# Layer 0 of a spectral convolution: two PSUM banks for the Hilbert rows, base bank first, and the low half by TensorE and ScalarE

## The reference

```python
# layer 0, on g = _gn(x)
X = jnp.fft.rfftn(g, axes=(-2, -1), norm='backward')
Yr = _rconv(Xr, wr) - _rconv(Xi, wi) + b_real[:, None, None]
Yi = _rconv(Xr, wi) + _rconv(Xi, wr) + b_imag[:, None, None]
x = x + jnp.fft.irfftn(lax.complex(Yr, Yi), axes=(-2, -1), norm='backward')
# layer 1, on g = _gn(x)
x = x + mean filter of 15 x 15 (g)
```

## Time and profile before

| | |
|---|---|
| median of 3 runs | 3912.32 us (3907.86 to 3915.44) |
| the profiled execution's own time | 3906.01 us |
| its span | 3904.2 us |
| busy: TensorE, VectorE | 3305.6 us (85%), 3271.4 us (84%) |
| busy: GpSimd, ScalarE | 2633.2 us (67%), 1926.4 us (49%) |

### The profile page before, as it was taken

One profiled execution on the slowest core, in us unless ns is written; L12 is line 12 of the kernel. 1 busy time (PEld: TensorE's weight loads), 2 busy tenths in 40 slices (PEclk: granted clock), 3 DMA queues, 4 the chain that ended last, 5 costly groups with the idle time before them and its releaser, 6 DMA issues.

```text
span 3904.2 us, 116132 instructions
## 1 busy us (share of the span) xinstructions
PE 3305.6 (85%) x38496; PEld 2354.2 (60%) x38496; DVE 3271.4 (84%) x6894; ACT 1926.4 (49%) x3262; POOL 2633.2 (67%) x2177
## 2 busy tenths in 40 slices
PE   2189889897988979889798898989899888988978
PEld 1155576555765567555675556755576555765567
DVE  7889977898778988789787997789977898888976
ACT  0067633675336752466425763267633675236742
POOL 5078853987539866498646885388853987639864
PEclk8599999999999999999999999999999999999999
DMA  6555556554765538655475554755466553765534
GB/s 158 182 96 120 100 175 193 108 120 80 222 166 114 119 79 244 145 117 118 117 233 112 120 117 139 224 100 120 96 185 188 112 120 77 229 163 115 118 82 136
DMA packets 785614, 542.42 MB, mean 139 GB/s; under 512 B 655216, under 2 KB 730576, under 8 KB 772944
## 3 DMA queue, kind: packets, MB, share of 16 engines
q1 hardware_dynamic: 762832, 420.23, 46.7%
q10 hardware_dynamic: 22400, 117.46, 10.8%
HBM read 256.31 MB, written 146.80 MB: 103 GB/s over the span
## 4 chain that ended last, share of the span: by engine, by line
PE 62%; DVE 16%; issue 12%; POOL 2%; DVEq 2%; ACT 2%; SPq 1%; DMA 1%; ACTq 1%; POOLq 0%
PE p L555 23%; PE h_ps L664 14%; PE h_ps L466 7%; PE p L690 6%; DVE ob_all L1147 5%; PE p L505 5%; PE p L562 2%; PE h_ps L555 2%; DVE ob_all L1141 2%; DVE ob_all L1228 2%; ACT arena L733 1%; PE p L474 1%; DVE ob_all L979 1%; DVEq L1167 1%; DVE stat L968 1%
## 5 line engine op out<-in xcount | busy, mean ns | idle before, releaser
L555 PE MATMUL p<-arena,bd_all 64*64 64x512 f16 x16896 | 1208.4, 378 | 207.3 <-DVE ob_all L1147 163.4
L555 PEld LDWEIGHTS p<-arena,bd_all 64*64 64x64 f16 x16896 | 675.9, 106 | 572.6 <-issue 336.0
L1296 POOL TENSOR_TENSOR arena<-arena 128x512 f16<-128x512 f32 x512 | 592.3, 1157 | 426.6 <-ACT arena L766 407.2
L1355 POOL TENSOR_TENSOR arena<-img 128x512 f32<-128x512 f32 x392 | 498.6, 1273 | 460.9 <-PE h_ps L664 438.6
L733 ACT ACTIVATE arena<-h_ps 128x512 f16<-128x512 f32 x512 | 305.7, 597 | 835.0 <-PE h_ps L664 599.6
L1303 POOL TENSOR_TENSOR ob_all<-ob_all,img 128x512 f32<-128x512 f32 x512 | 663.4, 1296 | 45.8 <-DVE ob_all L1141 45.8
L1306 POOL TENSOR_TENSOR ob_all<-ob_all 128x512 f32<-128x512 f32 x512 | 654.1, 1278 | 40.1
L773 ACT ACTIVATE arena<-h_ps 128x512 f16<-128x512 f32 x512 | 304.9, 595 | 622.3 <-PE h_ps L466 622.3
L664 PE MATMUL h_ps<-bd_all,arena 128*128 128x128 f32 x3584 | 539.6, 286 | 0.0
L1212 DVE TENSOR_TENSOR arena<-h_ps,arena 128x512 f16<-128x512 f32 x512 | 353.4, 690 | 205.0 <-ACT arena L733 203.8
L1141 DVE SCALAR_TENSOR_TENSOR ob_all<-p,bias_c,cosw 128x256 f32<-128x256 f32 x1024 | 448.0, 479 | 89.6 <-PE p L555 62.5
(11 more groups left out here) (162 smaller groups left out, 4551.8 us busy)
## 6 DMA issues: line engine op xcount, KB each, us to landing
out<-ob_all SPq DMA_DIRECT2D x512, 256.0 KB, 4.1
bd_all<-bd_dram SPq DMA_DIRECT2D x512, 192.0 KB, 2.3
img<-in_x ACTq DMA_DIRECT2D x168, 512.0 KB, 6.7
img<-in_x ACTq DMA_DIRECT2D x112, 256.0 KB, 4.5
wrap_mat<-tab_wrap_h SPq DMA_DIRECT2D x512, 32.0 KB, 2.0
img<-in_x SPq DMA_DIRECT2D x24, 512.0 KB, 24.1
bd_dram<-ob_all SPq DMA_DIRECT2D x16, 768.0 KB, 3.5
arena<-arena SPq DMA_TRANSPOSE x512, 2.7
```

The lines of the kernel that those rows point to most:

```text
L555: m = mm(bank[out_half * HP:(out_half + 1) * HP, :], bd[s % RB][rows, 6 * lm + (j if own else j + 1), :], part, start=opens and i3 == 0, s ...
L1296: G.tensor_tensor(gp[s][:, 1, :], g32, gp[s][:, 0, :], ALU.subtract).then_inc(g_split, 1)
L1355: G.tensor_tensor(diff[u % 2], img[:, u + R, :], img[:, u - R - 1, :], ALU.subtract).then_inc(moved, 1)
```

## The change

Five edits, all in layer 0:

1. The Hilbert rows alternate between two banks, `h_ps[:, 0]` and the new `h_odd` (the bank that was `xt_ps`).
2. The low half of a Hilbert row: before, VectorE computed (bank x scale - high part). Now TensorE adds -32768 times the high part to the bank with one matmul of 128x128 by 512 columns (`less_high`), and ScalarE copies what is left with a scale (`low_hilbert`). TAB_SCALE becomes 32768.
3. `g32` has two buffers, so `normalise` waits for the split of the row before the last, not of the last.
4. `mix` takes the base bank first: rounds 0 to 3 are p0 (row n opens, row n-1 closes), rounds 4 to 6 open p1 and p2, rounds 7 to 9 close them. The waits for t1_done and t2_done move from round 0 to round 4, those for p1_half and p2_half both to round 7, the one for p0_half to round 0.
5. `front_hilbert` waits for `h_split` of one row earlier.

```diff
-TAB_SCALE = 65536.0
+TAB_SCALE = 32768.0
+        "less_tab16": -TAB_SCALE * eye
...
-                                   start=(half == 0 and i == 0), stop=(half == 1 and i == 2))
+                                   start=(a == 0 and half == 0 and i == 0), stop=False, skip_group_check=True)
...
-            def front_hilbert(b, i, s):
+            def front_hilbert(b, i, s, first):
                 n = b * T + i * NG + s
                 pe.wait_ge(xt_in[s % 2], 32 * (b * (T // 2) + i * (NG // 2) + s // 2 + 1))
-                pe.wait_ge(h_split, PRIMED + n)
-                hilbert(lambda a: h_ps[:, 0, a * HALF:(a + 1) * HALF], xT[s % 2], HALF).then_inc(h_made, 1)
+                if first * NG + s >= 1:
+                    pe.wait_ge(h_split, PRIMED + n - 1)
+                hilbert(lambda a: hrow_ps[s % 2][:, a * HALF:(a + 1) * HALF], xT[s % 2], HALF).then_inc(h_made, 1)
+
+            def less_high(n, s):
+                pe.wait_ge(h_kept, n + 1)
+                mm(hrow_ps[s % 2], tb["less_tab16"][:], hp[s % RB][:, 0].rearrange("p a j -> p (a j)"),
+                   start=False, stop=True, skip_group_check=True).then_inc(h_less, 1)
...
                 def front(i, s, first):
+                    less_high(b * T + i * NG + s, s)
                     if first * NG + s + 1 < T:
-                        front_hilbert(b, i + (s + 1) // NG, (s + 1) % NG)
+                        front_hilbert(b, i + (s + 1) // NG, (s + 1) % NG, first + (s + 1) // NG)
...
                     def lower(r):
                         if r < 3:
-                            m = half_terms(p1[:], 2, r, 0, True, False)
-                            if r == 2:
-                                m.then_inc(p1_half, 1)
-                        elif r < 6:
-                            half_terms(p0[s % RB], 0, r - 3, 0, True, False)
-                        elif r == 6:
+                            half_terms(p0[s % RB], 0, r, 0, True, False)
+                        elif r == 3:
...
                             wrap_terms(0, False).then_inc(p0_half, 1)
+                        elif r < 7:
+                            m = half_terms(p1[:], 2, r - 4, 0, True, False)
+                            if r == 6:
+                                m.then_inc(p1_half, 1)
                         else:
-                            if r == 7:
-                                pe.wait_ge(p2_half, n + 1)
-                                pe.sem_inc(mix_step, 1)
                             m = half_terms(p2[:], 4, r - 7, 0, False, True)
...
                     def upper(r):
+                        if r < 4:
+                            if first * NG + s > 0:
+                                late_base((s - 1) % NG, (r,))
+                        elif r < 7:
+                            m = half_terms(p2[:], 4, r - 4, 1, True, False)
+                            if r == 6:
+                                m.then_inc(p2_half, 1)
                         else:
-                            if r == 5:
-                                pe.wait_ge(p1_half, n + 1)
-                                pe.sem_inc(mix_step, 1)
-                            m = half_terms(p1[:], 2, r - 5, 1, False, True)
+                            m = half_terms(p1[:], 2, r - 7, 1, False, True)
+                            if r == 9:
                                 m.then_inc(p1_ready, 1)
...
-                    pe.wait_ge(t1_done, PRIMED + n)
-                    pe.wait_ge(t2_done, PRIMED + n)
+                    if first * NG + s > 0:
+                        pe.wait_ge(p0_half, n)
                     pe.sem_inc(mix_step, 1)
                     for r in range(10):
+                        if r == 4:
+                            pe.wait_ge(t1_done, PRIMED + n)
+                            pe.wait_ge(t2_done, PRIMED + n)
+                            pe.sem_inc(mix_step, 1)
+                        if r == 7:
+                            pe.wait_ge(p2_half, n + 1)
+                            pe.wait_ge(p1_half, n + 1)
+                            pe.sem_inc(mix_step, 1)
                         lower(r)
                         upper(r)
...
+                def low_hilbert(n, s):
+                    act.wait_ge(h_less, n + 1)
+                    nc.scalar.activation(hp[s % RB][:, 1], halves(hrow_ps[s % 2]), ACT.Identity,
+                                         scale=1.0 / TAB_SCALE).then_inc(h_split, 1)
...
-                def low_hilbert(n, s):
-
-                    dve.wait_ge(h_kept, n + 1)
-                    V.scalar_tensor_tensor(hp[s % RB][:, 1], halves(h_ps[:, 0]), 1.0 / TAB_SCALE, hp[s % RB][:, 0],
-                                           ALU.mult, ALU.subtract).then_inc(h_split, 1)
```

More of the change, by code:

```diff
@@ L138, in tables @@
         "to_virtual": tov, "from_virtual": fromv,
-        "ident16": eye, "band16": box,
+        "ident16": eye, "band16": box, "less_tab16": -TAB_SCALE * eye,
         "stack_virtual": stackv.reshape(NV, P), "wrap_h16": wrap.reshape(T, P, P),
@@ L171, in build @@
         piece = [arena[:, i * W:(i + 1) * W] for i in range(16)]
-        g32 = piece[0]
         gp_flat = [piece[1 + s].bitcast(F16) for s in range(NG)]
@@ L198, in build @@
                for i in range(2)]
+        g32_more = sb("g32_more", [P, W])
+        g32 = [piece[0], g32_more[:]]
         xT_more = sb("xT_more", [P, W])
@@ L217, in build @@
         sc = sb("sc", [P, 28])
-        xt_ps = ctx.enter_context(nc.psum_tensor("xt_ps", [P, 8, P], F16))
+        h_odd = ctx.enter_context(nc.psum_tensor("h_odd", [P, W], F32))
         h_ps = ctx.enter_context(nc.psum_tensor("h_ps", [P, 2, W], F32))
@@ L225, in build @@
         uv_ps, c_ps = p0[2], p0[3]
-        uvT_ps = xt_ps[:].rearrange("p k m -> p (k m)").bitcast(F32).rearrange("p (k m) -> p k m", k=4)
+        hrow_ps = [h_ps[:, 0], h_odd[:]]
+        uvT_ps = h_odd[:].rearrange("p (k m) -> p k m", k=4)
         c_tab = h_ps[:, 1, 0:3 * P].rearrange("p (i t a) -> p i t a", i=3, a=2)
@@ L252, in build @@
         xt_in = [sem(f"xt_in{s}") for s in range(2)]
-        g_done, g_split, h_made, h_kept, h_split = (
-            sem("g_done"), sem("g_split"), sem("h_made"), sem("h_kept"), sem("h_split"))
+        g_done, g_split, h_made, h_kept, h_less, h_split = (
+            sem("g_done"), sem("g_split"), sem("h_made"), sem("h_kept"), sem("h_less"), sem("h_split"))
         p1_half, p2_half, p0_half = sem("p1_half"), sem("p2_half"), sem("p0_half")
@@ L539, in layer0 @@
                 m.then_inc(c_made, 1)
-                front_hilbert(b, 0, 0)
+                front_hilbert(b, 0, 0, 0)
                 pe.wait_ge(v_rows, b + 1)
@@ L760, in normalise @@
                     row = parity(img[:, i * NG + s, :])
-                    if first > 0:
-                        act.wait_ge(g_split, PRIMED + n)
+                    if first * NG + s > 0:
+                        act.wait_ge(g_split, PRIMED + n - 1)
                     nc.scalar.activation(halves(gp[s][:, 0, :]), row, ACT.Identity, bias=sc[:, 9:10], scale=sc[:, 8:9])
-                    if first == 0:
-                        act.wait_ge(g_split, PRIMED + n)
-                    nc.scalar.activation(halves(g32), row, ACT.Identity,
+                    nc.scalar.activation(halves(g32[s % 2]), row, ACT.Identity,
                                          bias=sc[:, 9:10], scale=sc[:, 8:9]).then_inc(g_done, 1)
@@ L813, in slot @@
                     t = first * NG + s
+                    low_hilbert(n, s)
                     if 0 < t and t + 3 < T:
@@ L1094, in layer0 @@
                 V.tensor_tensor(vrow[0:NV], vbase[0:NV], t1[0:NV], ALU.add).then_inc(v_rows, 1)
-                def low_hilbert(n, s):
-                    dve.wait_ge(h_kept, n + 1)
-                    V.scalar_tensor_tensor(hp[s % RB][:, 1], halves(h_ps[:, 0]), 1.0 / TAB_SCALE, hp[s % RB][:, 0],
-                                           ALU.mult, ALU.subtract).then_inc(h_split, 1)
-                low_hilbert(b * T, 0)
                 dve.wait_ge(c_made, b + 1)
@@ L1179, in slot @@
                         finish_row(n - 2, i * NG + s - 2, (s - 2) % NG, first - (s < 2))
-                    if t + 1 < T:
-                        low_hilbert(n + 1, (s + 1) % NG)
                 slot(0, 0, 0)
@@ L1295, in split_g @@
                     pool.wait_ge(g_done, n + 1)
-                    G.tensor_tensor(gp[s][:, 1, :], g32, gp[s][:, 0, :], ALU.subtract).then_inc(g_split, 1)
+                    G.tensor_tensor(gp[s][:, 1, :], g32[s % 2], gp[s][:, 0, :], ALU.subtract).then_inc(g_split, 1)
                 def add_terms(n, t, s, first):
@@ L1381 @@
     from concourse.bass_utils import run_bass_kernel_spmd
-    nc = bacc.Bacc("TRN2", target_bir_lowering=False, num_devices=1, dynamic_dma_scratch_size=8192)
+    nc = bacc.Bacc("TRN2", target_bir_lowering=False, num_devices=1, dynamic_dma_scratch_size=1024)
     arrays, args = {}, []
```

14 lines of the change are left out of this document (2 added, 12 removed).

## The result

The changed kernel takes 3988.67 us, median of 4 runs (3985.65 to 3993.17), against 3913.8 us before (4 runs, 3907.86 to 3915.44): 1.0195 times as long, 95% interval 1.0177 to 1.0213. It is slower by 75 us, where the prediction said 50 (3962 us). In the profiled executions the spans are 3983.8 and 3904.2 us.

A forecast was written before the change was run, and what follows sets the result against it. The prediction took a ring of mix and VectorE's reads as the bound. Cutting it leaves TensorE's 4.28 us slot; 4.0 + 1.4 + 0.9 = +6.3 us an image, times 8 = +50, gives 3962 us, 8 in 10 within 3912 to 4045.

The forecast's parts named there:

- What bounded the kernel before: Layer 0 slot: mix fills p1, VectorE reads, mix restarts, 4.21 us; TensorE's own work is 3.69 of 4.18.
- The half semaphores, +0.38 us: In mix, round 7 waits for round 6 to end and its semaphores: 0.41 + 0.18 - 0.215 us in every slot.
- w = 0.18: Wake of TensorE by its own semaphore before round 7: 0.14 plus 0.04 us, range 0 to 0.36.
- TensorE's own slot, 4.28 us: Layer 0 slot after the change: TensorE's work alone, with the gap behind round 6 and less_high, sums to 4.28 us.
- the +4.0 us of the loop: Loop of an image, 40 slots: 40 x (4.28 - 4.18) us more.
- ScalarE's copy, nothing: low_hilbert ahead of mix: 1.45 us from less_high's start, covered by 1.63 us, so no cost counted.
- rows 5 to 16, I take 0: Rows 5 to 16 of an image, now 49.3 us: no change, ends -2.2 and +0.8 us.
- the SP queue ... longer slots relax it: SP queue, nearly full at 4.2 us a slot: longer slots give it more room.
- ScalarE is late: Rival: ScalarE's copy comes 0.3 us late for mix, slot 4.58 us, +165 us, 4077 us; chance 0.14.
- The ends of an image: Start of an image: -1 and +1 us; end: p1 closes two rounds later and with the gap, about +0.9 us.
- not slower: Rival: the wait at round 7 is nearly free, slot 4.10 us, -50 us, 3862 us; chance 0.12.
- nothing moves: Rival: the new ring through p1 and p2 or GpSimd holds the slot at 4.2 us, 3912 us; chance 0.07.

The follow-up runs named there:

- before_one_more: Kernel before, with one more 128x128 by 512 matmul, result unused, between the Hilbert row and mix in every slot: 3905.34 us, ratio 0.9982.
- split_base_deep_wrap: Changed kernel with two base rounds between mix's opening and closing rounds, normalise and split_g four rows ahead, wrap_mat fetched from ScalarE's queue: 3823.74 us.
- old_order_deep: Changed kernel with mix's rounds and waits in the old order, and rows normalised and split four ahead instead of three: 3891.95 us, ratio 0.9947.
- split_base: Changed kernel with mix as two base rounds, three that open p1 and p2, two base rounds, three that close: 3898.85 us, ratio 0.9967.
- after_wrap: Changed kernel with wrap_mat's fetch taken out of the SP queue and issued by ScalarE two rows ahead: 3986.43 us, ratio 1.0190.
- deep: Changed kernel with normalise and split_g four rows ahead of mix instead of three: 3974.83 us, ratio 1.0164.
- split_base_deep: Changed kernel with two base rounds between mix's opening and closing rounds, and normalise and split_g four rows ahead: 3873.35 us, ratio 0.9907.

## Why the prediction was right, and where it was off

*What bounded the kernel before* held. The ring of mix and VectorE's two reads set the slot: a matmul put into the wait cost nothing (before_one_more), and the cut of the ring brought mix from 1.94 to 1.41 us behind the Hilbert row, in 487 of the 512 slots. With the ring cut and no gap in mix, slots fell to 3.91 us (split_base_deep_wrap), with the ring kept only to 4.12 (old_order_deep).

*The half semaphores, +0.38 us* held: 0.57 us between the starts of rounds 6 and 7 where the sum had 0.41 + 0.18 = 0.59. The four matmuls of round 6 start closer together than those of the earlier trace rows, so the round takes 0.39, and the wake is the 0.19 in the bracket. split_base shows that it is the distance and not the wait as such. The estimate of w = 0.18, by the row of VectorE's release less the stacked semaphore instructions, was good to 0.02, though 0.04 of it was an allowance that no row gave. The Trainium skill's tail, "TensorE: Matmul & The Clock Gate", section "The cost: per-tile semaphore tail", taken on top of my 0.41 + 0.14, gave an estimate of 0.65 for this distance and 0.06 us more for the slot, 4.34. The trace has neither: 0.57 and 4.30. It can't tell whether such a tail lies inside the 0.19.

*TensorE's own slot, 4.28 us* is 4.30 in most slots. The 0.02 are the first rounds, which take 1.32 us and not 1.29 behind a Hilbert row that they don't wait for. 40 slots of it and some longer ones turn the +4.0 us of the loop into +5.1.

*ScalarE's copy, nothing* was right about mix, which waits for it 13 times in all, 8.4 us, and only in an image's first or last mix. It was wrong about what is queued behind the copy. I had checked that ScalarE would be free when `less_high` ends, and not what the wait does to `normalise`, which stands after it in the queue. That is the step that failed: *rows 5 to 16, I take 0*, and with it *the SP queue ... longer slots relax it*. The queue itself was relaxed (after_wrap), but what it has to transpose came 2.1 us later. deep puts it at 14 us of the 29 that the sum was short (+79 against +50). The rival "ScalarE is late" had ScalarE late for mix, with slots of 4.58; it was late for the transposes instead, and the loop's slot stayed at 4.30.

*The ends of an image*: rows 0 to 5 took +1.2 us, where I had set -1 and +1 against each other, and the end -0.85 us where I had +0.9. I have not tested either. That the two nearly cancel is luck.

By parts, the 29 us are rows 0 to 5 (+10), rows 5 to 16 (+17), the loop (+9), the last seven (+7) and the end (-14). deep takes away 14 of the 17 and 4 of the 7, and its loop is 3 longer.

The other rivals: *not slower* needed a gap under 0.28 us and it was 0.36 (0.57 - 0.215); *nothing moves* needed a ring of 4.2 us, and mix waited for VectorE's reads in 8 of 512 slots only, 8.0 us in all, so in the others its ring was shorter than TensorE's 4.30.

## What to carry to other kernels

When a ring through another engine is cut, add up what the bound engine does alone before and after: here 3.69 us of 4.18 left room for 0.22, but not for 0.22 and a wait of the engine for its own matmuls. A wait of an engine for what it has just issued wants other work in between (here two rounds, 0.43 us). And when an instruction that waits is put at the head of an engine's queue, follow what stands behind it, as far as the DMA queues: it may be late for something that has nothing to do with the change, and it shows only where the slack there is least.

## What the runs showed of the hardware

- TensorE waiting for a semaphore that its own last four matmuls set: 0.57 us from start to start instead of 0.215; 0.36 with one round of four matmuls between; with two rounds it can't be seen.
- A matmul of 128x128 by 512 columns put into a wait of a slot cost nothing in 512 slots (0.9982 times the time).
- Two transposes and two fetches on the SP queue took 4.0 us a row where the queue hardly paused (split_base_deep); without the smaller fetch it kept up with slots of 3.91 us, with pauses.
- A transpose here lands 2.7 us after its issue in the median, but 31 to 46 of 1024 took over 4 us in the kernels before, changed and split_base_deep. It is the slow ones that the lead has to cover.
